# Masked cross-attention over 32 batches: the first key third projected a slot earlier, the masked values' second product a slot later

## What is computed

```python
q = _split_heads(Q @ W_q.T + b_q)
k = _split_heads(K @ W_k.T + b_k)
v = _split_heads(V @ W_v.T + b_v)
q, k, v = _nan_clamp(q), _nan_clamp(k), _nan_clamp(v)
...
logits = jnp.einsum('bhqd,bhkd->bhqk', q, k) * scale
logits = logits + bias
logits = jnp.where(mask == 0, -10000.0, logits)
probs = jax.nn.softmax(logits, axis=-1)
out = jnp.einsum('bhqk,bhkd->bhqd', probs, v)
return out @ W_o.T + b_o
```

## Time and profile before

| | us |
|---|---|
| median of three runs | 6049.69 (6029.98 to 6051.38) |
| the profiled execution, its own time | 6069.86 |
| its span | 6067.9 |

### The profile page before, as it was taken

One profiled execution on the slowest core, in us unless ns is written; L12 is line 12 of the kernel. 1 busy time (PEld: TensorE's weight loads), 2 busy tenths in 40 slices (PEclk: granted clock), 3 DMA queues, 4 the chain that ended last, 5 costly groups with the idle time before them and its releaser, 6 DMA issues. The chain is left out here.

```text
span 6067.9 us, 133226 instructions
## 1 busy us (share of the span) xinstructions
PE 5280.6 (87%) x51447; PEld 3803.5 (63%) x51447; DVE 4463.5 (74%) x9176; ACT 3193.1 (53%) x6024; POOL 1846.4 (30%) x1447
## 2 busy tenths in 40 slices
PE   3898898988679999987949999999999749999997
PEld 1777777777268887865924444444444427878885
DVE  7888888886367777762457777777777557777776
ACT  1666666666256666642224444444444326666663
POOL 5776767672122222202021111111111022222220
PEclk6999999999789999988979999999999879999998
DMA  5655555553267777742010000000000049888891
GB/s 126 132 122 131 126 128 126 126 128 80 51 128 140 139 135 142 141 84 101 22 33 26 16 15 15 15 15 15 15 15 10 8 101 156 159 163 162 161 156 28
DMA packets 369568, 545.00 MB, mean 90 GB/s; under 512 B 116084, under 2 KB 248310, under 8 KB 368806
## 3 DMA queue, kind: packets, MB, share of 16 engines
q1 hardware_dynamic: 366982, 533.81, 43.5%
q0 software_dynamic: 2048, 3.67, 0.2%
HBM read 413.45 MB, written 123.90 MB: 89 GB/s over the span
## 5 line engine op out<-in xcount | busy, mean ns | idle before, releaser
L698 DVE CUSTOM_DVE_ANT_0 attn_logits<-attn_scores,attn_shift 112x750 f32<-112x750 f32 x1024 | 945.8, 933 | 436.5 <-PE attn_scores L503 436.5
L616 ACT ACTIVATE attn_probs_t<-attn_pt 125x448 f32<-125x448 f32 x1536 | 829.4, 541 | 583.7 <-PE attn_pt L518 563.2
L518 PEld LDWEIGHTS attn_pt<-ident,attn_logits 112*125 112x125 f32 x6144 | 852.6, 189 | 180.0 <-issue 95.1
L518 PE MATMUL attn_pt<-ident,attn_logits 112*125 112x112 f32 x6144 | 921.4, 273 | 26.7 <-ACT attn_logits L607 23.8
L2385 PE MATMUL attn2k_pk<-attn_wk,attn_cn_t 128*125 128x512 f32 x1536 | 740.1, 604 | 39.8 <-ACT attn_cn_t L2451 36.6
L2396 PE MATMUL attn2k_pg<-attn_kn,attn_cn 125*128 125x512 f32 x1536 | 726.2, 595 | 4.5 <-ACT attn_gram L2459 2.3
L2504 DVE TENSOR_REDUCE attn_ss<-attn_sq 125x16 f32<-125x1024 f32 x384 | 467.0, 1216 | 245.3 <-ACT attn_sq L2478 245.0
L415 POOL CAST attn_k_parts<-xn_t 128x500 bf16<-128x500 f32 x192 | 206.3, 1075 | 1429.2 <-DVE xn_t L670 1429.2
L2478 ACT ACTIVATE attn_sq<-attn2k_pk 125x1024 f32<-125x1024 f32 x384 | 391.5, 1019 | 330.8 <-PE attn2k_pk L2385 330.6
L1230 ACT ACTIVATE attn_probs_t<-attn_pt 125x448 f32<-125x448 f32 x768 | 413.9, 539 | 278.2 <-PE attn_pt L1117 276.3
L2385 PEld LDWEIGHTS attn2k_pk<-attn_wk,attn_cn_t 128*125 128x125 f32 x1536 | 274.7, 187 | 400.6 <-issue 298.3
(11 more groups left out here) (371 smaller groups left out, 10444.3 us busy)
## 6 DMA issues: line engine op xcount, KB each, us to landing
attn_k_packed<-k_scratch SPq DMA_DIRECT2D x372, 375.0 KB
attn_k_packed<-k_scratch SPq DMA_DIRECT2D x408, 187.5 KB, 4.4
k_scratch<-attn_k_parts SPq DMA_DIRECT2D x64, 1125.0 KB
attn_ctx_t<-in_ctx_t SPq DMA_DIRECT2D x64, 750.0 KB
k_scratch<-attn_k_parts SPq DMA_DIRECT2D x96, 375.0 KB, 3.7
attn_ctx_t<-in_ctx_t SPq DMA_DIRECT2D x96, 250.0 KB, 4.6
attn_ctx<-in_ctx SPq DMA_DIRECT2D x32, 750.0 KB
attn_mask_in<-in_mask SPq DMA_DIRECT2D x192, 109.4 KB
```

The costliest lines, as they stand in the source:

```text
L518: last = pe.transpose(pt[(3 * at + t) % 2][0:KC, (c % 4) * PAIR:(c % 4 + 1) * PAIR], logits[:, at % 3, c * KC:(c + 1) * KC], g.ident[0:PAI ...
L616: act.activation(probs_t[0:KC, p // 4, 4 * t:4 * t + 4, (p % 4) * PAIR:(p % 4 + 1) * PAIR], pt[(3 * at + t) % 2][0:KC, 0:QUAD].rearrange(" ...
L698: dve.tensor_tensor_reduce(out=logits[:, at % 3, cols].rearrange("p (b k) -> p b k", b=2), in0=scores[h][0:PAIR, :, 0:QTR], in1=shift[:, n ...
```

## The change

In words, part by part:

- `keys(n + 3, 0)` is projected in slot 7 of batch n, and `keys(n + 2, 1)` and `keys(n + 2, 2)` in slots 0 and 1, where thirds 0, 1 and 2 of batch n + 2 were projected in slots 0, 1 and 2. ACT's `keep` moves along. The first third of batch 2 is projected ahead of the loop.
- The context third that this needs is loaded earlier in SP's queue: `load_ctx(n + 3, 0)` stands behind the store of the second key third, no longer with the other two.
- `side` is now written by `keys(n + 3, 0)` between `sums(n - 1)` and `out(n - 1)`. So `keys` with third 0 waits until DVE has read the sums (`attn_steps`), and `out(n - 1)` waits until ACT has emptied `side` (`raw_k_ready`). The wait on `y_copied` goes to third 1.
- DVE's `take` of the key thirds moves from slots 2, 3 and 4 to 1, 2 and 3, and `finite` from slots 1, 2 and 3 to 0, 1 and 2. The value parts stay where they were.
- The second group of `weigh_masked` moves from slot 1 to slot 2. `load_mask_t` waits for it.

```diff
--- before.py
+++ after.py
@@ -937,6 +937,8 @@
                     if n + 2 < B:
                         store_keys(n + 2, 0)
                         store_keys(n + 2, 1)
+                    if n + 3 < B:
+                        load_ctx(n + 3, 0)
                     if n + 1 < B:
                         load_keys(n + 1, 1, (0, 1, 2))
                     if n + 2 < B:
@@ -944,8 +946,8 @@
                     if n + 1 < B:
                         load_keys(n + 1, 1, (3, 4, 5))
                     if n + 3 < B:
-                        for i in range(3):
-                            load_ctx(n + 3, i)
+                        load_ctx(n + 3, 1)
+                        load_ctx(n + 3, 2)
                     if n + 2 < B:
                         load_mask(n + 2, 0)
                         load_queries(n + 2)
@@ -1054,6 +1056,9 @@
                     pe.wait_ge(ctx_in[i], 16 * (n + 1))
                     if i == 0:
                         wait(pe, raw_v_ready, 3 * n)
+                        if n > 3:
+                            pe.wait_ge(attn_steps, 3 * (n - 4) + 1)
+                    if i == 1:
                         wait(pe, y_copied, n - 3)
                     wait(pe, raw_k_ready, 3 * n + i)
                     pe.matmul(side[:, 0:THIRD], wk[:], ctx_t[:, third(i)], start=True, stop=True).then_inc(k_turned, 1)
@@ -1086,6 +1091,8 @@
 
                 def out(n):
                     pe.wait_ge(attn_ready, n + 1)
+                    if n + 4 < B:
+                        pe.wait_ge(raw_k_ready, 3 * (n + 4) + 1)
                     for i in range(4):
                         last = pe.matmul(side[:, 0:S], wo[:, i, :], attn[:, i * S:(i + 1) * S],
                                          start=(i == 0), stop=(i == 3))
@@ -1154,6 +1161,7 @@
                         keys(n, i)
                     for i in range(3):
                         values(n, i)
+                keys(2, 0)
 
                 FIRST, SECOND = range(0, CH // 2), range(CH // 2, CH)
 
@@ -1167,16 +1175,18 @@
                         score(n, p, 1)
                         if some:
                             turn(*prior, 1)
-                        if p < 3 and n + 2 < B:
-                            keys(n + 2, p)
+                        if p < 2 and n + 2 < B:
+                            keys(n + 2, p + 1)
+                        if p == 7 and n + 3 < B:
+                            keys(n + 3, 0)
                         if 3 <= p < 6 and n + 2 < B:
                             values(n + 2, p - 3)
                         if p == 6 and n > 0:
                             sums(n - 1)
                         if some:
                             turn(*prior, 2)
-                        if p in (0, 1) and n > 0:
-                            weigh_masked(n - 1, p)
+                        if p in (0, 2) and n > 0:
+                            weigh_masked(n - 1, p // 2)
                         if p in (2, 3) and n > 0:
                             weigh(n - 1, 1, FIRST if p == 2 else SECOND)
                         if p == 5 and n > 0:
@@ -1257,6 +1267,7 @@
                 count(0)
                 for i in range(3):
                     keep(1, i)
+                keep(2, 0)
                 for n in range(B):
                     for p in range(HP):
                         prior = (n, p - 2) if p > 1 else (n - 1, p + HP - 2)
@@ -1268,8 +1279,10 @@
                                 exp(*prior, t)
                             if t < 2 and last[0] >= 0:
                                 lower(*last, t)
-                            if t == 1 and p < 3 and n + 2 < B:
-                                keep(n + 2, p)
+                            if t == 1 and p < 2 and n + 2 < B:
+                                keep(n + 2, p + 1)
+                            if t == 1 and p == 7 and n + 3 < B:
+                                keep(n + 3, 0)
                         if p == 1 and n > 0:
                             weigh_share(n - 1)
                         if p == 4 and n > 0:
@@ -1471,10 +1484,10 @@
                 for n in range(B):
                     for p in range(HP):
                         shifted(n, p, 0)
-                        if p > 1 and n + 2 < B:
-                            take(n + 2, p - 2)
-                        if 0 < p < 7 and n + 2 < B:
-                            finite(n + 2, p - 1)
+                        if p in (1, 2, 3, 5, 6, 7) and n + 2 < B:
+                            take(n + 2, p - 1 if p < 4 else p - 2)
+                        if p in (0, 1, 2, 4, 5, 6) and n + 2 < B:
+                            finite(n + 2, p if p < 3 else p - 1)
                         if p in (0, 2, 4) and n + 1 < B:
                             mark(n + 1, p // 2)
                         if p == 5:
```

## The result

The changed kernel takes 6255.9 us, median of 4 runs (6254.1 to 6271.7); the kernel before 6049.8 us (6030.0 to 6051.4). The ratio is 1.0356, 95% interval [1.0335, 1.0376]: **slower by 206 us**. Forecast were 6175 us and a range of 6085 to 6240; the direction was right, the size too small, and the time lies 16 us above the range.

What follows compares the result with a forecast made beforehand. PE and DVE hold each other up in turn, 42.83 us a batch. Seven pieces sum to 47.1 us, 4.3 more; over 29 batches 125 us on the median of 6049.7 give 6175 us, range 6085 to 6240.

Steps and rivals of the forecast that it cites:

- x to `shifted(1, 0)`: From `normalise`'s reciprocal (x) through slot 0: `out` waits for ACT's `keep`, slot 0 unchanged; 12.8 us, was 10.44.
- To `shifted(2, 0)`: Slot 1, now with a take and a `finite` but without 48 PE matmuls; 5.1 us, was 4.87.
- To the end of `mark`: Slot 2, the same kinds of operation with the second third for the first; 4.8 us, as before.
- To the landing: From `mark`'s end, the third third's cast waits for the first third's store: 7.7 us, DVE waiting some 4.7.
- To `keep_values`: From the third third's cast, through a `shifted`, to the end of `keep_values`; 2.7 us.
- To `take_values`: To slot 6's take: DVE alone would need 11.36 us, POOL's chain becomes the limit; 12.1 us, was 13.35.
- To the reciprocal: From `take_values` in slot 6 to the next reciprocal of `normalise`; 1.9 us, as before.
- the even load wins: DVE's idle stretches take in the moved work and nothing new waits; 2.2 us less per batch, 5985 us; chance 0.05.
- The waits only trade places: Landing nearer 3.3 us and no moved operation held up; 42.7 us a batch, no change, 6050 us; chance 0.08.
- The store gets later still: Mask loads go out in one burst, POOL holds up moved operations; halfway 49.3 us a batch, 6238 us; chance 0.07.
- The first of the two rules beside the rows: VectorE and GpSimd share a port pair, so every moved `finite` could be held up; about 2 us per batch.
- The rule on a transfer's time: About 2.0 us plus bytes over 436 GB/s: 375 KB store in 2.9 us, total about 6100 us.

Runs made afterwards that it cites:

- e4: The change with the second group of `weigh_masked` put back from slot 2 to slot 1; 6238.1 us, ratio 1.0332.
- e1: The change with the store of the first key third moved ahead of the mask loads in SP's queue; 6091.8 us, ratio 1.0099.
- e5: The change with the first third's store ahead of the mask loads and ACT's early `keep` ahead of both `lower`s in slot 7; 6010.1 us, ratio 0.9953.
- e2: The change with ACT's `keep` of the early third placed ahead of both `lower`s of slot 7; 6209.1 us, ratio 1.0281.
- e10: The kernel before with only the second group of `weigh_masked` moved from slot 1 to slot 2; 6052.1 us, ratio 1.0025.
- e9: The change with the first third's store placed between the loads of mask_t and of the mask's last third; 6186.5 us, ratio 1.0253.
- e6: e5 with POOL's query `blocks` moved behind the last two value guards; 6088.5 us, ratio 1.0088.
- e3: The change with DVE's take of the third key third put back from slot 3 to slot 4; 6089.6 us, ratio 1.0082.

## Why the prediction was wrong in size

The path was right: both waits came, in their places, and the direction with them. **Two steps failed.** The landing of the first third's store was taken at 5.5 us and is 6.6; this is the largest term, 1.2 us a batch. And PE's work was taken at full clock behind the two waits that the prediction itself put in, where it runs at 1.2 GHz behind the stall in every batch and behind `out` in 8 of 23. Behind `out` that costs 0.5 us a batch in the mean; behind the stall, up to 0.8, it is in part argued.

By the prediction's own steps: for the batch shown, which takes 50.70 us where the sum said 47.1, and in brackets the mean of the 22 batches between 212 and 1340 us, 50.36 in all.

1. *x to `shifted(1, 0)`: 14.2 us [13.3], forecast 12.8.* `out` starts at 524.79, x + 5.91, where x + 5.8 was forecast: the mechanism and its place were right. What failed here is "5.15 through slot 0, whose work is unchanged": in this batch it takes 6.49 (525.70 to 532.19). From 526.88 to 530.35 PE runs at 1.2 GHz: four score matmuls step by 1.25 us instead of 0.65, the four turns of 528.13 by 0.82 instead of 0.42, the projection by 1.40 instead of 0.86, together 1.5 us. This holds for the 8 batches in which the clock falls there, which take 14.2 to 14.7 us; the other 14 take 12.5 to 13.0, as forecast.
2. *To `shifted(2, 0)`: 5.17 [5.16], forecast 5.1.* Right. The held-up `finite` falls in slot 0, under PE's wait.
3. *To the end of `mark`: 5.30 [5.29], forecast 4.8.* `mark` takes 1.45 us instead of 0.81, in every batch; here it ends at 543.55, 0.29 us behind an operation of POOL with two inputs that started just ahead of it. Within the bounds.
4. *To the landing: 8.52 [8.91], forecast 7.7.* **The mis-sized term.** The issue came at the forecast 2.19 us; the landing takes 6.2 us here and 6.61 in the median where 5.5 was taken. I saw that mask_t would go out right ahead of the store and put its cost, "up to 1.5", into the upper bound alone; with mask_t out early (e4) the store lands in 5.56 us, so the missing 1.05 are mask_t's. DVE's wait is 6.19 us in the mean where 4.7 was forecast.
5. *To the end of `keep_values`: 2.65 [2.65], forecast 2.7.* Right.
6. *To `take_values`: 12.53 [12.87], forecast 12.1.* In this batch POOL's chain and DVE's own work end together, 12.44 us behind the copy's end at 554.72. So they do in 8 of the 22 batches. In the other 14 POOL is done after 11.86 us and DVE alone takes 13.07, where 11.36 was priced for it: behind the stall it waits for PE twice, 2.0 us in the batch of 609.81:

```profile
609.81 0.69 DVE L1377 TENSOR_TENSOR y_t<-attn_side,attn_bv 125x512 f32<-125x512 f32 x1 [0.74 <-PE attn_side L1070]
...
611.88 1.00 DVE L1424 CUSTOM_DVE_ANT_0 x_sb<-attn_scores,attn_bias,attn_floor 112x750 f32<-112x750 f32 x1 [1.26 <-PE attn_scores L1114]
```

   PE leaves the stall at 1.2 GHz there; how much of the 2.0 us is the clock was not tried apart. POOL as the limit of this piece was thus wrong for most batches.
7. *To the reciprocal: 2.33 [2.15], forecast 1.9.* The `finite` there takes 0.82 us instead of 0.41 in this batch.

So of the 3.3 us that the sum lacked in the mean 1.2 are piece 4 (the landing), 0.8 piece 6 (DVE behind the stall), 0.5 each piece 1 (the clock behind `out`) and piece 3 (`mark`), and 0.3 the rest. The experiments cut the loss of 7.56 us a batch in another way: 5.67 for the store (the change to e1) and 3.02 for `out` (e1 to e5), or 2.17 for `out` first (e2) and 6.52 for the store behind it, each with the clock that it costs, less 1.13 that the change wins (e5 against before).

The range failed by its upper end. It went half of the way to the upper bounds, as if each of them were unlikely; two of the terms behind them, mask_t ahead of the store and operations held up by POOL, were in every batch.

The rivals: *the even load wins* had the right mechanism and a condition that did not hold. With both waits gone (e5) the batch is 41.67 us, 1.13 below before, where 2.2 were priced; the time is 6010 and not 5985. *The waits only trade places* is near to e10, 1.70 us for 1.25. *The store gets later still* came nearest in the end, 50.24 us against its 49.3, with the landing as its reason and the clock as one that it didn't have.

The first of the two rules beside the rows, on operations that POOL holds up, priced about 2 us a batch. Pieces 2 and 3 came 0.55 above the forecast together, with `mark` as the main part. Its reading of the rows left one thing out: the `finite` of 0.42 us at 523.45 met no two-input operation of POOL, but it did run beside one with one input, and was not held up by it. POOL, before:

```profile
522.23 2.09 POOL L1000 TENSOR_SCALAR attn_clean_late<-xn_t 128x500 f32<-128x500 f32 x1
```

The rule on a transfer's time, weighed beside piece 4: no store of before was as short as its estimate of 2.9 us. e1 and e5 show it: 2.9 and 3.0 us, where nothing was issued on the queue in the 5.4 us ahead of the store, and 7.9 behind mask_t in e9. The Trainium skill (DMA: Bandwidth & Descriptors, section Queues, rings and completion order) says that each DMA engine takes the descriptors of a ring in order. The trace is in line with it, since 375 KB issued behind 328 KB land 4.7 us later in the median; but no trace has the landing of mask_t itself, so the order is not shown.

## What to carry to other kernels

When a change brings the use of a buffer forward, look up where its release stands in the in-order queue that makes it, and what each entry ahead of it waits for: moving one store ahead of the entries that wait took back 5.67 of 7.56 us a batch. Price a new wait of PE with what may follow it too: behind the stall of about 5 us the matmuls ran at half rate in every batch, behind the wait of 1.3 to 1.8 us in 8 of 23, and taking that wait of 1.5 to 1.7 us away gained 2.2 to 3.0. Then look at more than one batch: the one shown here was not the usual one. Before moving an operation on POOL, see which two-input operation of DVE will then start beside it.

## What the runs showed that was not expected

- DVE's comparison of 392 ns takes 3015 ns in all 26 batches of e6, where POOL's `blocks` starts 0.04 us ahead of it (2.62 us a batch).
- A 375 KB store lands in 2.9 us with nothing issued on its queue in the 5.4 us before it (e1), in 7.9 us 0.32 us behind a load of 328 KB on the same queue (e9).
- A wait of PE for ACT of 1.3 to 1.8 us is followed by matmuls at 1.2 GHz in 8 of 23 batches of the change, though not at once: at 525.70 a score matmul still takes 0.33 us, at 526.88 it takes 0.52. In e3 PE waits up to 3.0 us at a time, and from 480 to 750 us the granted clock is 1.00. What decides between the two is not shown.
- At the same work the granted clock of the first attention went from 0.91 (the change) to 1.00 (e5) by two edits that only move a store and a copy.
